# Transformer block with self- and cross-attention: one batch per loop turn over five staggered batches, and probabilities turned by the DMA queue

## The reference

```python
h = _layernorm(x, g1, b1)
x = _attention(h, h, wq1, wk1, wv1, wo1, bo1) + x          # 16 heads of 64, 256 keys
h = _layernorm(x, g2, b2)
x = _attention(h, cond, wq2, wk2, wv2, wo2, bo2) + x       # 16 heads of 64, 120 keys
h = _layernorm(x, g3, b3)
a, gate = jnp.split(h @ w_ff1 + b_ff1, 2, axis=-1)
x = a * jax.nn.gelu(gate, approximate=False) @ w_ff2 + b_ff2 + x
```

## Time and profile before

| | |
|---|---|
| median of 3 runs | 3031.53 us (3029.98 to 3031.58) |
| profiled execution, span of the page | 3030.7 us (no other time of that execution is listed) |
| TensorE (PE) busy | 94% |
| VectorE (DVE) busy | 82% |
| ScalarE (ACT) busy | 74% |
| GpSimd (POOL) busy | 36% |
| DMA after the first slice | 2 to 13 GB/s |

### The profile page before, as it was taken

One profiled execution on the slowest core, in us unless ns is written; L12 is line 12 of the kernel. 1 busy time (PEld: TensorE's weight loads), 2 busy tenths in 40 slices (PEclk: granted clock), 3 DMA queues, 4 the chain that ended last, 5 costly groups with the idle time before them and its releaser, 6 DMA issues.

```text
span 3030.7 us, 84452 instructions
## 1 busy us (share of the span) xinstructions
PE 2836.3 (94%) x28943; PEld 2222.4 (73%) x28943; DVE 2477.9 (82%) x5160; ACT 2248.0 (74%) x6573; POOL 1078.6 (36%) x2358
## 2 busy tenths in 40 slices
PE   0899999999999999999999999999999999999999
PEld 0577777777777777777777877778777777777777
DVE  7887888878788787987878888787888878878787
ACT  2685868868687685977868688686877858678686
POOL 4342433424243242432424334242432424334242
PEclk9999999999999999999999999999999999999999
DMA  5000000000000000000000000000000000000000
GB/s 207 5 9 9 12 2 13 8 13 9 9 10 3 13 9 9 11 3 13 9 12 9 2 13 9 13 9 10 10 4 13 9 9 10 3 13 9 9 2 9
DMA packets 32245, 41.73 MB, mean 14 GB/s; under 512 B 6140, under 2 KB 29848, under 8 KB 31384
## 3 DMA queue, kind: packets, MB, share of 16 engines
q1 hardware_dynamic: 31768, 35.61, 3.7%
HBM read 27.21 MB, written 8.39 MB: 12 GB/s over the span
## 4 chain that ended last, share of the span: by engine, by line
PE 58%; ACT 19%; DVE 11%; issue 9%; POOL 1%; DMA 1%; DVEq 0%; SPq 0%; ACTq 0%; POOLq 0%
PE group_ps L909 13%; ACT arena L523 12%; PE group_ps L973 11%; PE group_ps L985 10%; PE group_ps L946 6%; PE group_ps L914 6%; PE score_ps L931 4%; PE group_ps L963 4%; ACT arena L533 3%; PE score_ps L996 2%; DVE stat L617 2%; ACT arena L513 2%; PE group_ps L879 1%; DVE peak L760 1%; DVE arena L724 1%
## 5 line engine op out<-in xcount | busy, mean ns | idle before, releaser
L457 POOL TENSOR_SCALAR arena<-arena,share 128x120 f32<-128x120 f32 (+1 forms) x2048 | 837.5, 429 | 1321.4 <-DVE share L768 1316.8
L523 ACT ACTIVATE arena<-score_ps,shift,sc 128x120 f32<-128x120 f32 (+1 forms) x2048 | 1047.4, 582 | 3.8 <-DVE shift L764 2.3
L743 DVE SCALAR_TENSOR_TENSOR arena<-group_ps,arena 128x256 f16<-128x256 f32 (+3 forms) x1152 | 625.2, 563 | 188.4 <-ACT arena L513 150.8
L523 ACT ACTIVATION_READ_ACCUMULATOR arena<-score_ps,shift,sc 128x1 f32 x2048 | 567.8, 279 | 0.0
L513 ACT ACTIVATE arena<-group_ps 128x512 f16<-128x512 f32 (+2 forms) x640 | 407.1, 641 | 187.0 <-PE group_ps L909 159.0
L775 DVE TENSOR_TENSOR arena<-group_ps,arena 128x512 f16<-128x512 f32 (+1 forms) x768 | 499.0, 681 | 29.6 <-ACT arena L533 26.1
L533 ACT ACTIVATE arena<-group_ps 128x512 f16<-128x512 f32 (+1 forms) x768 | 464.2, 696 | 75.2 <-PE group_ps L946 75.2
L760 DVE TENSOR_REDUCE peak<-score_ps 128x4 f32<-128x480 f32 (+1 forms) x512 | 474.9, 927 | 0.0
L946 PE MATMUL group_ps<-ident,arena 128*128 128x128 f32 (+1 forms) x3072 | 431.6, 278 | 11.4 <-POOL arena L457 11.4
L946 PEld LDWEIGHTS group_ps<-ident,arena 128*128 128x128 f32 (+1 forms) x3072 | 336.1, 140 | 77.0 <-DVE arena L775 30.0
L909 PE MATMUL group_ps<-arena,wq 128*128 128x256 f16 x3072 | 388.1, 279 | 0.0
(11 more groups left out here) (94 smaller groups left out, 3126.3 us busy)
## 6 DMA issues: line engine op xcount, KB each, us to landing
xin<-in_x SPq DMA_DIRECT2D x32, 256.0 KB, 2.8
out<-xres SPq DMA_DIRECT2D x32, 256.0 KB, 3.9
cin<-in_ctx SPq DMA_DIRECT2D x32, 90.0 KB, 2.2
arena<-in_ctx SPq DMA_DIRECT2D x1, 2880.0 KB, 12.9
arena<-in_L_xattn_wq SPq DMA_DIRECT2D x2, 1024.0 KB, 19.4
arena<-in_L_xattn_wo SPq DMA_DIRECT2D x2, 1024.0 KB, 15.9
arena<-in_L_xattn_w_ff SPq DMA_DIRECT2D x1, 2048.0 KB, 16.6
arena<-in_L_xattn_wk SPq DMA_DIRECT2D x1, 1024.0 KB, 17.2
```

The costliest lines, as they stand in the source:

```text
L457: nc.gpsimd.tensor_scalar(rows, rows, share[:, p % 4, 2 * h + t:2 * h + t + 1], 2.0 ** BOUND, ALU.mult, ALU.mult).then_inc(probs_ready, 1)
L523: ins = nc.scalar.activation(probs[:, p % 4, h, t, 0:K], score_ps[:, p % 2, h, t * K:t * K + K], ACT.Exp, scale=score_scale[a], bias=shift ...
L743: nc.vector.scalar_tensor_tensor(dst, src, factor, high, ALU.mult, ALU.subtract).then_inc(group_done, 1)
```

## The change

**Loop.** There are no slots A and B any more. An iteration handles each step once, each step for batch `i + lead`; the lead, 0 to 4, stands behind a `+` in the new table. Leads 4 and 3 hold self-attention, 2 cross-attention, 1 the feed-forward part, 0 its end and the store. Iterations -4 to 31 are run, those whose batch does not exist leave steps out: -4 to 0 and 28 to 31 are written out straight, 1 to 27 are a hardware loop. Every kind of group has its own semaphores, and buffers exist per attention instead of per slot, mostly as rings of two.

**Probabilities.** POOL still normalises. Then ACT writes the high half straight from SBUF (`high`), POOL the low half (`low`), into one block for each pair, and one DMA on the SP queue turns the block with both halves (`move`): 128 x 2048 f16 for self-attention, 128 x 1024 f16 for cross-attention (keys padded to 128). The PE transposes and the PSUM evictions L533 and L775 are gone.

**Others.** Each attention has one score bank of its own. `out` is two groups of 128x512 over half of the heads each, with two residual additions; `ff2` is four groups in the ring with four additions; the SBUF copy of `ff1` is gone; `gelu` is a ring of two; layer norm of batch 0 is no longer done ahead of the weights.

```diff
 TABLE = """
+move2.5+1 q2.0+2 move2.6+1 high2.7+1 low2.7+1 mix1.0+3 mix2.5+1 move1.1+3 mix2.6+1 move2.7+1 scores1.4+3
+scores2.0+2 max2.0+2 high1.2+3 low1.2+3 max1.4+3 high1.3+3 v1.3+3 low1.3+3 exp2.0+2 share2.0+2 mix1.1+3
+ff2.1.0+0 ff2.1.1+0 store+0 norm2.0+2 move1.2+3 scores2.1+2 max2.1+2 exp1.4+3 mix2.7+1 share1.4+3 norm1.4+3
...
+max1.6+3 share2.2+2 exp2.3+2 share2.3+2 k2.1+2 q2.3+2 low1.4+3 exp1.6+3 bias1+3 norm2.2+2 norm2.3+2 load+4
+stats1+4 ff1.0+1 ff1.1+1 share1.6+3 gate.0+1 gate.1+1 ff1.2+1 ff1.3+1 gate.2+1 gate.3+1 inner.0+1 scores1.7+3
+max1.7+3 rows1+4 norm1.6+3 move2.0+2 ff1.4+1 high2.2+2 gate.4+1 low1.5+3 move1.4+3 high1.6+3 ff1.5+1 ff1.6+1
+gate.5+1 low1.6+3 low2.2+2 ff1.7+1 inner.1+1 gate.6+1 gate.7+1 ctx+3 turn1+4 hlow1+4 scores2.4+2 max2.4+2
+out1.0+3 exp1.7+3 share1.7+3 norm1.7+3 mix1.4+3 clow+3 exp2.4+2 share2.4+2 mix2.0+2 q1.0+4 k1.0+4 k1.1+4
...
+        probs = {a: carve(2 * HT * KEYS[a]).rearrange("p (r t h k) -> p r t h k", r=2, t=TT, h=2) for a in (1, 2)}
+        halves = {a: carve(2 * HT * PADDED[a]).bitcast(F16).rearrange("p (r t i h k) -> p r t i h k", r=2, t=TT, i=2, h=2)
+        probsT = {a: carve(2 * HT * PADDED[a]).bitcast(F16).rearrange("p (r b n) -> p r b n", r=2, b=BLOCKS[a]) for a in (1, 2)}
...
+            def move(bt, a, j):
+                sp.wait_ge(probs_low[a], nth(bt, 8, j))
+                if j >= 2 or not is_first(bt):
+                    sp.wait_ge(full[f"mix{a}"], nth_ago(bt, j, 2, 8))
+                sp.dma_start_transpose(probsT[a][:, j % 2], flat[a][:, j % 2]).then_inc(moved[a, j % 2], 16)
...
+            def low_half(bt, a, j):
+                pool.wait_ge(probs_high[a], nth(bt, 8, j))
+                nc.gpsimd.tensor_tensor(two, probs[a][:, j % 2], one, ALU.subtract).then_inc(probs_low[a], 1)
...
+            def exponentials(bt, a, j):
+                act.wait_ge(shift_ready[a], nth(bt, 8, j))
+                if j >= 2 or not is_first(bt):
+                    act.wait_ge(probs_low[a], nth_ago(bt, j, 2, 8))
...
+            def high_half(bt, a, j):
+                act.wait_ge(probs_ready[a], scaled_nth(bt, 8, j, 4))
+                if j >= 2 or not is_first(bt):
+                    act.wait_ge(moved[a, j % 2], ...)
+                nc.scalar.activation(halves[a][:, j % 2, :, 0, :, 0:K], probs[a][:, j % 2], ACT.Copy).then_inc(probs_high[a], 1)
...
+            def scores(bt, a, j):
+                if j or not is_first(bt):
+                    pe.wait_ge(exp_done[a], nth_ago(bt, j, 1, 8))
...
-            def turn_probs(turn, p):
-                            ins = nc.tensor.transpose(bank[0:K, at:at + P], probs[:, p % 4, h, t, k * P:k * P + K], ident[:])
...
+            def mix(it, bt, step):
+                pe.wait_ge(moved[a, j % 2], scaled_nth(bt, 4, j // 2, 16))
```

More of the change, by code:

```diff
@@ L85 @@
[L85 to L98, removed]
@@ L103, in read_step @@
+COUNT = {**PROJ, "turn1": 1, "turn2": 1, "turn3": 1, "ctx": 1, "mix1": 8, "mix2": 8, "out1": 2, "out2": 2,
+         "ff1": 8, "ff2": 4}
+RING = 4
 def read_step(text):
[L104 to L111, removed]
@@ L137, in places @@
[L137 to L152, removed]
@@ L153 @@
[L153 to L168, removed]
@@ L171, in of_pair @@
-def of_pair(p):
-    return p // PAIRS % 2, p // (2 * PAIRS) + 1, p % PAIRS
+    name, lead = text.split("+")
+    name, *part = name.split(".")
+    part = [int(i) for i in part]
+    if name in PROJ:
+        step = ("proj", name, *part)
+    elif name not in ("ff1", "ff2") and name[-1].isdigit():
+        step = (name[:-1], int(name[-1]), *part)
+    else:
+        step = (name, *part)
+    return step, int(lead)
+ORDER = [read_step(text) for text in TABLE.split()]
+LEAD = dict(ORDER)
+ORDER = [step for step, _ in ORDER]
@@ new lines, with group_kind, is_group @@
+MAXLEAD = max(LEAD.values())
+def group_kind(step):
+    if step[0] == "proj":
+        return step[1], step[2]
+    if step[0] in ("turn", "mix", "out"):
+        return f"{step[0]}{step[1]}", (*step[2:], 0)[0]
+    if step[0] == "ff2":
+        return "ff2", 2 * step[1] + step[2]
+    return step[0], (*step[1:], 0)[0]
+def is_group(step):
+    return step[0] in ("proj", "turn", "ctx", "mix", "out", "ff1", "ff2")
+NGROUP = sum(is_group(step) for step in ORDER)
+assert NGROUP % RING == 0 and NGROUP == sum(COUNT.values())
@@ new lines, in active, with nth, scaled_nth, before @@
+def active(i, batches):
+    return [step for step in ORDER if 0 <= i + LEAD[step] < batches]
+def nth(b, n, k):
+    turn, base = b
+    return base * n + k + 1 if turn is None else turn * n + (base * n + k + 1)
+def scaled_nth(b, n, k, each):
+    turn, base = b
+    return each * (base * n + k + 1) if turn is None else turn * (each * n) + each * (base * n + k + 1)
+def before(b):
+    return b[0], b[1] - 1
+def is_first(b):
+    return b[0] is None and b[1] == 0
+def ago(b, j, back, n):
+    return (b, j - back) if j >= back else (before(b), j - back + n)
@@ new lines, in store @@
+            def store(bt):
+                sp.wait_ge(done["ff2"], nth(bt, 4, 3))
+                sp.dma_start(row_of(out_view, bt), x4[:]).then_inc(stored, 16)
+            for it, steps in iterations(sp):
+                for step in steps:
+                    bt = batch(it, step)
+                    if step[0] == "load":
+                        next_rows(bt)
+                    elif step[0] == "cload":
+                        next_ctx(bt)
+                    elif step[0] == "move":
+                        move(bt, *step[1:])
+                    elif step[0] == "store":
+                        store(bt)
```

906 lines of the change are left out of this document (424 added, 482 removed).

## The result

The changed kernel takes 2975.4 us in the median (2969.4 to 2978.4), against 3031.2 before: ratio 0.981, 95% interval 0.980 to 0.983. It is 1.9% faster where 8% was forecast. The profiled execution has a span of 2967.3 us.

The account below looks back on a forecast made before the run. PE was taken to bound the kernel: 77.1 us of work, 2.2 and 2.1 of waits and 0.6 of coupling make 82 us a batch; 92 + 2624 (32 batches) + 69 = 2785 us, range 2700 to 3110 (forecast's own 2700 to 2860).

Parts of the forecast that it names:

- Part 1: Transposes leave PE: a batch loses 11.6 us of PE work, 77.1 us remain.
- Part 3: Other engines' work a batch: ACT 72.5 us with its loop edge, DVE 59.2, POOL 61.5, all staying under PE's time.
- Part 5: Added waits between engines and on moves: mostly hidden, 0.6 us for tighter coupling, giving 82 us a batch.
- Part 2: PE's remaining waits: loop edge 2.2 us once a batch plus 2.1 us of others, giving 81.4 us a batch.
- No clock to win or lose: PE's granted clock: read as at its upper level, 2.4 GHz, in every slice, so nothing to gain or lose.
- Part 4: DMA transposes: 4.5 us a self-attention move, 2.8 a cross-attention one, 58 us a batch one at a time, under 81.4.
- The queue: Rival, SP queue becomes the bound at `move`: slower than today if a self-attention move costs over 7.5 us; chance 0.20.
- Part 6: Ends of the run: 92 us come first, and 69 us are lost in the first three and last three iterations.
- coupled engines: Rival: late POOL steps delay ACT, then a mix; 5 us a batch more, 2945 us in all; chance 0.18.

Follow-up runs that it names:

- b_no_low: Changed kernel with POOL's subtraction for the low halves cut to two elements a partition, low halves staying zero; 2751.0 us, ratio 0.908 to before.
- g_one_input: Changed kernel with POOL's subtraction replaced by two POOL instructions of one input and the same size; 3612.0 us, ratio 1.192 to before.
- f: Changed kernel with POOL's subtraction in four pieces and the loop written out straight; 2743.7 us, ratio 0.905 to before.
- c_no_move: Changed kernel with each DMA transpose replaced by a plain DMA of 16 elements a row; 2951.1 us, ratio 0.974 to before.

## Why the prediction was wrong in size

- **Part 1** held: 77.1 us of matmuls a batch, and b_no_low shows 77.1. The DMA transposes took them off PE as forecast.
- **Part 3 is the step that failed**, at its sum for DVE (59.2). It took every row of DVE from a kernel in which POOL had no long two-input instruction in its loop but the bias, and added POOL's 28.8 us of them as if they ran on their own. They lengthened DVE to 70.2; without them it is 59.5. The text even chose 2.4 us over 2.0 for POOL "with DVE at work" and did not ask what DVE pays. DVE still stayed below PE: not its total made the loss but the place of the lengthened instructions, ahead of a gate that PE waits for. The Trainium skill states the rule, in "SBUF — State Buffer", section "Who interferes with whom": DVE and GpSimd share a pair of ports, locked by one of them at a time, for the whole instruction, and on this chip a `tensor_reduce` never contends. The trace agrees: L787 at 2.32 us beside a subtraction and 0.67 without, the maxima at 1212 as before. For POOL instructions of one input the measurement is more lenient than the rule: a shift within one is held in two stretches and passes between them (g_one_input).
- **Part 5** had 0.6 us for coupling. The gate, late behind this, cost a pause of 2.56 us and mostly 1.7 us of slower matmuls. Taking the subtraction away gives 87.5 - 79.9 = 7.6 us an iteration; cutting it in four gives 5.0 of that.
- **Part 2** had 2.2 us for the edge. The pause was 3.2 in the mean, over the 3 us that the prediction gave as its sign of being wrong here, and a batch got back 87/32 = 2.7 us in all without the loop. Why it is 1 us longer is open: it is 2.3 without the subtraction and about as short without the transposes. "No clock to win or lose" was wrong too, and for the kernel before already: a digit of 9 on the page stands for anything from 90%, the mean was 0.993, and 11 of 15 jumps were followed by a lowered clock. In the kernel after it is 0.961, from two such places an iteration; in f's window it is 1.00. Of PE's 80.7 us, 3.6 are this.
- **Part 4** held. A move took 4.3 us in the median, 4.5 and 2.8 were taken, and mixes waited 4.4 us for it in the whole span. The queue was not the bound. What the prediction made of the Trainium skill's figure for one block (251 us a batch) did not come about at this size.
- **Part 6** held: 2967 - 32 x 87.5 = 167 us lie outside 32 iterations, against 161.
- Without the failed step the sum was close: b_no_low took 2751 us, 1.2% under the forecast (2785), with 79.9 us a batch for 82. That is partly luck: it had PE idle for 2.8 us a batch, where parts 2 and 5 had 4.9. Of the rivals, "coupled engines" came nearest, with 87 us a batch and 2945; but it named late POOL steps ahead of ACT, and the wait ran by DVE's gate.

## What to carry to other kernels

When work moves to POOL as an instruction with two SBUF inputs, charge it to DVE too, and look at which DVE step a late end would hold up; cut it into pieces of about 0.7 us before thinking of another engine. That was worth 5% here, with POOL busier than before it; cutting on, to 446 ns, lost 1.2% of it again. When an engine at its bound jumps back once a turn, time the kernel written straight before halving the turn, and look at the granted clock behind several jumps, not behind one.

## What the runs showed of the hardware

- POOL subtracts 128 x 1024 in 2157 ns in one instruction and in 4 x 703 = 2812 in four, whereas its `tensor_scalar` over the same pattern takes 2775 ns, more than twice the forecast for g_one_input, although the one of the softmax takes 480 ns for 256.
- While POOL runs a subtraction with two SBUF inputs, a DVE instruction on SBUF data waits for its end (45 of 45 shifts, to 0.04 us, in the kernel after); POOL's `tensor_scalar` of 2775 ns holds a shift that starts in its first 0.8 us or its last 1.0 us, and none between (g_one_input).
- A pause of PE of 2.0 to 3.5 us was followed by a lowered clock in most cases, not in all: 11 of 15 at the jumps before, 22 of 26 and 23 of 29 after. Each time this cost about 1.7 us. No run here shows what decides.
- Jumps cost more than their pause in the earlier trace rows: 5.1 us each in the kernel before against 2.2. The Trainium skill, "Runtime: NRT & Kernel Launch", section "Instruction fetch mechanics", says that a jump can force a fetch of instructions. No run here shows whether the pause is that; they show that it goes away without the loop, and that it is shorter, 2.3 us for 3.2, without POOL's subtraction (b_no_low), and about as much without the DMA transposes (c_no_move). By what either lengthens it stays open.
